# First layer's expert blocks of 128 rows instead of 256, and register reads four at a time

## The chip, the cores and the metric

The kernel runs on one core of one Trainium2 chip, in one launch. The metric is the device time of an execution in microseconds (us). The trace is that of one profiled execution.

## What is computed

The reference is a small vision tower of two layers: a patch embedding of 128 images (64 patches and a class token each, 65 x 128 = 8320 tokens of 128 numbers), then per layer an attention-like mixing and a mixture of experts of which each token uses two. The change lies in the first layer's experts, which compute:

```
xt = x.reshape(-1, d)                                   # 8320 tokens, d = 128
sel = jax.nn.sigmoid(xt @ expert_sel.T)                 # E = 32 experts
sel_val, sel_idx = jax.lax.top_k(sel, TOP_K)            # TOP_K = 2
w = jnp.zeros((T, E)).at[jnp.arange(T)[:, None], sel_idx].add(sel_val)
h = jax.nn.relu(jnp.einsum('td,edh->teh', xt, keys))    # hidden 128
out = jnp.einsum('teh,te,ehv->tv', h, w, values)
```

The second layer has 16 experts of hidden size 512 with biases and an exact gelu, again two a token.

## The kernel before, in words

The kernel runs in stages. In the first one groups of 520 tokens are embedded, mixed by attention and routed. Routing gives each of a token's two choices a row (132 numbers: the normalized token, the place where its result belongs, gate, spread and mean), and POOL scatters these rows into a list per expert in DRAM, `lists_L` (line 1551). When all are counted, DVE and PE make a table of blocks, `t_entry`, one integer a block that holds the expert and the first row. Since an expert's count is seldom a multiple of the block size, one block's worth of pad rows is written behind each expert's list: `pads`, lines 402 to 416, half of the experts by SP and half by ACT, each position read from the table `t_fr` into a register with `value_load` (line 412).

Then come the **expert blocks**. `Layer` fixes their size (256 rows for both layers) and their number: the most blocks that 16640 rows can need, rounded up to the unroll of 8, which is 96 in the first layer and 80 in the second. The number does not depend on the data; blocks beyond the last real one work on a dummy place. Eight buffers (`wblk`, `xblk`, `yblk`, index u) are used in turn. Every engine runs the same loop over blocks, 8 to a round, in program order:

- SP (`load`, lines 427 to 436) reads the block's table entry into a register (line 429), derives expert and row by register arithmetic, waits until the results that left buffer u eight blocks earlier have landed (`y_out[u]`), and issues two DMAs: the expert's weights (line 433, 128 KB in the first layer) and the block's rows (line 434, 132 KB). Both count up `blk_in[u]`.
- PE (`step`) does, for block i: transposes of block i + 2 (`t1`, line 626), which wait for `blk_in`; the first product of block i + 1 (`t2`, line 637); the second product of block i (`t3`, line 656). As PE works in order, `t3` of block i stands behind the transposes of block i + 2.
- ACT copies the transposed tile out of PSUM (line 796).
- DVE does relu of block i + 1 (line 1335), restores the rows of block i from spread and mean (line 1356, one instruction for each 128 rows) and adds the gated product (line 1375, one for each 128 rows).
- POOL (`send_results`) scatters the results into `results_L` (line 1565, one indirect DMA for each 128 rows), which counts up `y_out[u]`.

A block has Q = block / 128 such sub-tiles, 2 before. In the second layer relu is replaced by gelu and the first product is split in three passes (line 641).

After the blocks SP waits for all results (line 459) and loads them for the middle stage (line 441), which mixes, normalizes and routes for the second layer; then the second layer's pads and blocks, and the sum of each token's two results to the output.

Of the kernel before, what the change touches and what calls it, by code (L numbers as in the profile page):

```python
# [39 lines left out]
TOP = 2  # L40
# [126 lines left out]
class BlockSignals:  # L167


    def __init__(self, sem, i0, j0, y0, first=None):  # L170
        self.i0, self.j0, self.y0 = i0, j0, y0
# [12 lines left out]

def build(nc, a, out):
    ctx = ExitStack()
    with ctx:
# [156 lines left out]
        K = {"L0": BlockSignals(sem, 0, 0, 0)}  # L344
        K["L1"] = BlockSignals(sem, L0.blocks, L0.blocks // NB, 16 * L0.Q * L0.blocks // NB, K["L0"])

# [70 lines left out]
        def sp_blocks(sp, l):  # L417
# [8 lines left out]

            def load(u, j):
# [18 lines left out]
        def _(sp):  # L446
# [11 lines left out]
            for u in range(NB):  # L458
                sp.wait_ge(K["L0"].y_out[u], 16 * L0.Q * L0.blocks // L0.unroll)

# [5 lines left out]
            for u in range(NB):  # L466
                sp.wait_ge(K["L1"].y_out[u], K["L1"].y0 + 16 * L1.Q * L1.blocks // L1.unroll)

# [8 lines left out]
        def _(pe):  # L477
# [129 lines left out]
            def expert_blocks(l):  # L607
# [14 lines left out]
                def t1(u, j, n):  # L622
                    b, jj = turn(u, n, j)
                    pe.wait_ge(k.blk_in[b], 32 * (k.j0 + jj + 1))
# [38 lines left out]
                rounds = l.blocks // U  # L663
# [4 lines left out]
                def step(u, j, last):  # L668
                    if not (last and u + 2 >= U):
                        t1(u, j, 2)  # L670
                    if not (last and u + 1 >= U):
                        t2(u, j, 1)
                    t3(u, j, 0)
                for u in range(U):
                    step(u, 0, False)
                with pe.Fori(1, rounds - 1) as j:
                    for u in range(U):
                        step(u, j, False)
                for u in range(U):
                    step(u, rounds - 1, True)  # L680


# [89 lines left out]
        def _(act):  # L772
# [131 lines left out]
            def expert_blocks(l):  # L904
# [25 lines left out]
                def high(u, j, n):  # L930
                    i = U * j + u + n
                    act.wait_ge(k.blk_in[(u + n) % U], 32 * (k.j0 + j + (u + n) // U + 1))
# [9 lines left out]
                for u in range(U):  # L942
                    for f, lead in works:
                        f(u, 0, lead)
                with act.Fori(1, l.blocks // U - 1) as j:
                    for u in range(U):
                        for f, lead in works:
                            f(u, j, lead)
                for u in range(U):
                    for f, lead in works:  # L950
                        if u < U - lead:
                            f(u, l.blocks // U - 1, lead)
# [81 lines left out]
        def _(dve):  # L1034
# [290 lines left out]
            def expert_blocks(l):  # L1325
# [34 lines left out]
                def gated(u, j):  # L1360
# [4 lines left out]
                    dve.wait_ge(k.y_out[u], k.y0 + 16 * l.Q * j)  # L1365
                    y = ps[:, 6 + p2, 0:l.Q * D].rearrange("p (q d) -> p q d", q=l.Q)
                    if l.FC > 1:
                        dve.tensor_tensor(yblk[u][:, :, :], y,  # L1368
# [3 lines left out]
                        y = yblk[u][:, :, :]  # L1372
# [8 lines left out]
                def step(u, j, last):  # L1381
                    if not (last and u + lead >= U):
# [4 lines left out]
                for u in range(U):  # L1387
                    step(u, 0, False)
                with dve.Fori(1, l.blocks // U - 1) as j:
                    for u in range(U):  # L1390
                        step(u, j, False)
                for u in range(U):
                    step(u, l.blocks // U - 1, True)
# [239 lines left out]
```

## Time and profile before

| what | value |
|---|---|
| runs of the kernel | 1355.03, 1352.3, 1352.3 us; median 1352.3 |
| the profiled execution | 1354.35 us |
| its span, first to last instruction | 1352.6 us |
| mean granted TensorE clock | 0.836 |
| PE busy | 1024.7 us, 76% |
| DVE busy | 914.6 us, 68% |
| POOL busy | 700.3 us, 52% |
| ACT busy | 499.8 us, 37% |
| moved by DMA | 226.72 MB, mean 168 GB/s |

The busy shares are means over stages that differ much; what binds a stage is seen in that stage alone. The page's "idle before" gives what an engine waited for, and a name with q behind it (SPq) is an engine's own sequencer, which issues DMAs and is not counted as busy.

### The profile page before, as it was taken

What the parts mean: (1) busy time and instruction counts of PE and PEld (TensorE: products, weight loads), DVE (VectorE), ACT (ScalarE), POOL (GpSimd) and SP (SyncE); (2) the same over time, 40 slices, a digit from 0 to 9 for tenths busy, and PEclk for the clock granted to TensorE, in tenths of its full rate; (3) what the DMA queues carried; (4) which work ended last, traced back from release to release, by engine and by line L of the source; (5) the groups of instructions that cost most, each with busy time, mean ns of one, the idle gap of its engine ahead of it and who ended that gap; (6) DMA issues with size and microseconds to landing.
All of it is one profiled execution on the core that took longest, in us unless ns stands there. A gap on an engine that the chain in (4) does not pass through costs nothing.

```text
span 1352.6 us, 23759 instructions
## 1 busy us (share of the span) xinstructions
PE 1024.7 (76%) x6272; PEld 851.1 (63%) x6272; DVE 914.6 (68%) x3546; ACT 499.8 (37%) x1416; POOL 700.3 (52%) x698
## 2 busy tenths in 40 slices
PE   6999999999996326666665377777619999999920
PEld 3576666666665225555554367677618999999920
DVE  1587787787786426666665488888727888888832
ACT  1344444344353001111111255555405666656610
POOL 1033553553453517777777047777763555555520
PEclk8999999999997567888787666666658999999965
DMA  9656656566600265444442323332147777777648
GB/s 372 253 194 215 215 209 210 212 212 209 217 24 21 83 176 149 147 144 141 147 146 67 80 71 73 82 80 60 42 129 262 246 244 249 249 235 244 218 106 273
DMA packets 113697, 226.72 MB, mean 168 GB/s; under 512 B 21144, under 2 KB 87771, under 8 KB 107266
## 3 DMA queue, kind: packets, MB, share of 16 engines
q1 hardware_dynamic: 79424, 181.38, 41.5%
q0 software_dynamic: 21504, 34.73, 8.4%
q10 hardware_dynamic: 12714, 9.99, 2.5%
q8 instruction: 21, 0.34, 0.1%
q14 instruction: 34, 0.28, 0.1%
HBM read 180.32 MB, written 51.66 MB: 172 GB/s over the span
## 4 chain that ended last, share of the span: by engine, by line
PE 59%; DMA 11%; DVE 8%; issue 8%; ACT 6%; POOL 5%; SPq 2%; POOLq 0%; DVEq 0%; ACTq 0%
PE ps L656 11%; PE ps L641 9%; PE ps L493 7%; PE ps L735 5%; PE ps L490 5%; POOL results_L L1565 4%; PE ps L738 4%; DMA xin<-results_L 4%; DMA results_L<-xin 3%; DMA xin<-lists_L 3%; ACT ntok L983 2%; PE ps L554 2%; PE ps L626 2%; PE ps L511 2%; PE ps L538 2%
## 5 line engine op out<-in xcount | busy, mean ns | idle before, releaser
L1551 POOL DMA_INDIRECT lists_L<-rows,slots x270 | 302.0, 1119 | 358.5 <-issue 358.2
L1565 POOL DMA_INDIRECT results_L<-xin x352 | 343.6, 976 | 219.8 <-DVE xin L1375 142.7
L656 PEld LDWEIGHTS ps<-xin,hTb 128*128 128x128 f32 x1664 | 221.8, 201 | 9.7 <-DVE hTb L1335 0.3
L656 PE MATMUL ps<-xin,hTb 128*128 128x128 f32 x1664 | 225.7, 284 | 0.1
L493 PE MATMUL ps<-xin,w_emb 128*128 128x512 f32 x384 | 181.4, 605 | 10.3 <-DMA xin<-in_x_main 10.3
L626 PE MATMUL ps<-ident,xin 128*128 128x128 f32 x352 | 82.7, 322 | 134.8 <-DMA xin<-lists_L 134.5
L925 ACT ACTIVATE hTb<-ps,xin 128x256 f32<-128x256 f32 x320 | 125.6, 476 | 107.0 <-PE ps L641 107.0
L626 PEld LDWEIGHTS ps<-ident,xin 128*128 128x128 f32 x352 | 43.2, 156 | 155.5 <-DMA xin<-lists_L 155.2
L796 ACT ACTIVATE xTb<-ps 128x256 f32<-128x256 f32 x96 | 36.9, 384 | 238.9 <-PE ps L626 238.9
L1335 DVE TENSOR_SCALAR hTb<-ps 128x256 f32<-128x256 f32 x96 | 40.7, 424 | 109.8 <-PE ps L637 109.7
L493 PEld LDWEIGHTS ps<-xin,w_emb 128*128 128x128 f32 x384 | 68.2, 193 | 68.9 <-issue 58.6
L1356 DVE TENSOR_SCALAR xin<-xin 128x128 f32<-128x128 f32 x352 | 111.2, 366 | 0.0
L735 PE MATMUL ps<-ntok,w_emb 104*104 104x128 f32 x160 | 49.1, 431 | 67.0 <-ACT ntok L983 67.0
L641 PE MATMUL ps<-x_hi,x_lo 128*128 128x256 f32 x320 | 97.8, 306 | 0.0
L641 PE MATMUL ps<-x_lo,x_hi 128*128 128x256 f32 x320 | 91.2, 285 | 0.0
L641 PE MATMUL ps<-x_hi 128*128 128x256 f32 x320 | 90.9, 284 | 0.0
L735 PEld LDWEIGHTS ps<-ntok,w_emb 104*104 104x104 f32 x160 | 37.9, 290 | 68.8 <-ACT ntok L983 43.3
L637 PE MATMUL ps<-xTb,xin 128*128 128x256 f32 x192 | 74.4, 478 | 0.0
L1375 DVE SCALAR_TENSOR_TENSOR xin<-ps,xin 128x128 f32<-128x128 f32 x192 | 58.5, 346 | 12.5
L1368 DVE TENSOR_TENSOR xin<-ps,xin 128x256 f32<-128x256 f32 x80 | 34.0, 425 | 42.4 <-PE ps L656 42.3
L796 ACT ACTIVATE x_hi<-xin 128x512 fp32r<-128x512 f32 x80 | 51.7, 646 | 29.3 <-DMA xin<-lists_L 29.3
L641 PEld LDWEIGHTS ps<-x_lo,x_hi 128*128 128x128 f32 x320 | 62.1, 194 | 0.0
(196 smaller groups left out, 2204.7 us busy)
## 6 DMA issues: line engine op xcount, KB each, us to landing
xin<-in_x_main SPq DMA_DIRECT2D x48, 1536.0 KB, 6.9
xin<-in_w_L SPq DMA_DIRECT2D x80, 578.0 KB
xin<-lists_L SPq DMA_DIRECT2D x176, 132.0 KB
xin<-results_L SPq DMA_DIRECT2D x32, 520.0 KB
xin<-in_w_L SPq DMA_DIRECT2D x96, 128.0 KB
results_L<-xin POOLq DMA_INDIRECT x352
lists_L<-rows,slots POOLq DMA_INDIRECT x270
out<-xin ACTq DMA_DIRECT2D x16, 260.0 KB
```

Source lines behind the costliest of these rows:

```text
L490: mm = pe.matmul(psE[h], w[:, n, :], x[:, n, :], start=False, stop=False, skip_group_check=True)
L493: mm = pe.matmul(psE[h], w_emb[:, k, :], xin[h][c][:, n, :], start=(k == 0), stop=False, skip_group_check=True)
L626: mm = pe.transpose(ps[:, (u + n) % 2, q * 128:(q + 1) * 128], xblk[b][:, q, 0:D], ident[:, :])
L637: mm = pe.matmul(bank_h(p2, f), wblk[b][:, cols_f], xTb[p2][:, 0:n_tok], start=True, stop=True)
L641: mm = pe.matmul(bank_h(p2, f), w[p2][:, cols_f], x[p2], start=(n2 == 0), stop=(n2 == 2), skip_group_check=True)
L656: mm = pe.matmul(o, hTb[p2][:, f, q * 128:(q + 1) * 128], w2[:, f * D:(f + 1) * D], start=(f == 0), stop=(f == l.FC - 1))
L735: mm = pe.matmul(o, m[:, t, 0:ROWS], ntok[:, t, :], start=True, stop=(t == 0), skip_group_check=True)
L796: return act.activation(dst, src, ACT.Copy)
L925: ins = act.activation(hTb[p2][:, f, 0:l.block], ps[:, 2 + 2 * p2 + f // 2, f % 2 * l.block:(f % 2 + 1) * l.block], ACT.Gelu, bias=b1)
L1356: ins = dve.tensor_scalar(xblk[u][:, q, 0:D], xblk[u][:, q, 0:D], xblk[u][:, q, SPREAD:SPREAD + 1], xblk[u][:, q, MEAN:MEAN + 1], ALU.mult ...
L1551: pool.indirect_dma_start(out=lists[l.name], out_offset=bass.IndirectOffsetOnAxis(ap=slots_of(l, g, h)[:, t, k:k + 1], axis=0), in_=buf[:, ...
L1565: pool.indirect_dma_start(out=results[l.name], out_offset=bass.IndirectOffsetOnAxis(ap=xblk[u][:, q, PLACE:PLACE + 1].bitcast(U32), axis=0 ...
```

## The change

The first layer's blocks have 128 rows (Q = 1). Their number is no longer rounded up to a multiple of 8: it is 161 in the first layer (80 in the second, as before). The loops do a first round of 8, the inner rounds, and then the last whole round and the remaining block written out. Since 161 is no multiple of 8, the counts of the semaphores that both layers share are kept for each buffer. The block tables and the pad positions are read into registers four at a time, in both layers. In the second layer nothing else changes. A pad is now 128 rows in the first layer.

```diff
-        most = (TOKENS * TOP + experts * (block - 1)) // block
+        self.blocks = (TOKENS * TOP + experts * (block - 1)) // block
         self.unroll = unroll
-        self.blocks = -(-most // unroll) * unroll
+        self.rounds = self.blocks // unroll
+        self.turns = [len(range(u, self.blocks, unroll)) for u in range(unroll)]
...
-L0 = Layer(1, "L0", 32, 128, 256)
+L0 = Layer(1, "L0", 32, 128, 128)
...
         def rounds(eng, l, body):
 
-            for u in range(l.unroll):
-                body(u, 0)
-            with eng.Fori(1, l.blocks // l.unroll) as j:
-                for u in range(l.unroll):
+            U = l.unroll
+            for i in range(U):
+                body(i, 0)
+            with eng.Fori(1, l.rounds - 1) as j:
+                for u in range(U):
                     body(u, j)
+            for i in range(U * (l.rounds - 1), l.blocks):
+                body(i % U, i // U)
...
+        def several(engine, where, most):
+
+            return nc.values_load_multi_w_load_instructions(where, engines=[engine], min_val=0, max_val=most)[1]
...
             with eng.Fori(0, l.E // 8) as e:
-                for u in range(4):
-                    at = eng.value_load(tb.fr[0:1, bass.ds(half * (l.E // 2) + 4 * e + u, 1)], min_val=0,
-                                        max_val=l.E * l.room - l.block)
+                engine = mybir.EngineType.SP if half == 0 else mybir.EngineType.Activation
+                for at in several(engine, tb.fr[0:1, bass.ds(half * (l.E // 2) + 4 * e, 4)], l.E * l.room - l.block):
...
             def load(u, j):
                 i = l.unroll * j + u
-                entry = sp.value_load(tb.entry[0:1, bass.ds(i, 1)], min_val=0, max_val=l.E * l.step - 1)
+                if u % 4 == 0:
+                    n = min(4, l.blocks - i) if isinstance(i, int) else 4
+                    for m, value in enumerate(several(mybir.EngineType.SP, tb.entry[0:1, bass.ds(i, n)], l.E * l.step - 1)):
+                        held[m] = value
+                entry = held[u % 4]
                 e, r = entry // l.step, entry % l.step
 
-                sp.wait_ge(k.y_out[u], k.y0 + 16 * l.Q * j)
+                sp.wait_ge(k.y_out[u], k.y0[u] + 16 * l.Q * j)
```

On SP's queue, at the head of the first layer's inner loop, one block before reads (t_entry is the block table, xin_0 the weight buffer, xin_2 the row buffer, y_out the semaphore of the results that left the buffer):

```order
L429 TENSOR_LOAD t_entry
L429 ISA x2
L432 REGISTER_ALU
L433 ISA [waits y_out0]
L433 DMA xin_0<-in_w_L 128x256
L434 ISA
L434 DMA xin_2<-lists_L 128x264
L429 ISA
L429 TENSOR_LOAD t_entry
L429 ISA x2
L433 ISA [waits y_out1]
```

and now:

```order
L413 TENSOR_LOAD t_entry
L413 ISA x8
L451 REGISTER_ALU
L452 ISA [waits y_out0]
L452 DMA xin_0<-in_w_L 128x256
L453 ISA
L453 DMA xin_2<-lists_L 128x132
L452 ISA [waits y_out1]
L452 DMA xin_0<-in_w_L 128x256
L453 ISA
L453 DMA xin_2<-lists_L 128x132
```

A load with two ISA instructions (a bounds check and an assertion) stood before every block; now one load and eight of them stand before every fourth, and the row DMA has 132 instead of 264 numbers a partition.

On POOL's queue the first layer's scatters before (x16 is the first round, x2 one block of the loop, of which eight stand in a round):

```order
L1565 DMA results_L<-xin_2 16640x128 x16
L397 UNCONDITIONAL_BRANCH
L397 ISA
L1565 DMA results_L<-xin_2 16640x128 x2
L1562 REGISTER_ALU
```

and now:

```order
L1564 DMA results_L<-xin_2 16640x128 x8
L401 UNCONDITIONAL_BRANCH
L401 ISA
L1564 DMA results_L<-xin_2 16640x128
L1561 REGISTER_ALU
...
L1564 DMA results_L<-xin_2 16640x128 x9
```

One scatter a block stands where two stood, and nine blocks follow the loop.

## Rows read from the trace of the kernel before

**Rows 1.** Busy time by stage; the stages are stretches of the span in us

```profile
core 0: us, PE busy (x) PEld busy (x) DVE busy (x) ACT busy (x) POOL busy (x), PEclk, DMA share, GB/s
...
462.00:491.00 29.00, 1.29 (x8) 0.61 (x8) 2.36 (x14) 0.00 (x0) 9.94 (x10) 0.50 0.67 201
491.00:749.00 258.00, 160.26 (x768) 130.93 (x768) 151.06 (x484) 38.16 (x97) 187.28 (x192) 0.80 0.45 133
749.00:1010.00 261.00, 164.35 (x920) 158.13 (x920) 191.85 (x1142) 116.23 (x450) 160.11 (x160) 0.61 0.30 76
1010.00:1301.00 291.00, 277.72 (x2400) 277.06 (x2400) 230.64 (x640) 168.57 (x401) 156.34 (x160) 0.98 0.71 230
```

**Rows 2.** POOL's scatters: ns min/median/max, first and last start; as a group in 510:730

```profile
L1565 POOL DMA_INDIRECT results_L<-xin x192: 971/972/1300, 501.8 to 746.4; - x192
...
L1565 POOL DMA_INDIRECT results_L<-xin x173 | 168.4, 974 | 52.7 <-issue 47.3 <-DVE xin L1375 5.5
```

**Rows 3.** Waits (total, times, longest): PE in 491:749, SP in 510:730, SP in 1009:1305

```profile
PE ps L626 <- DMA xin<-lists_L: 111.0, 81, 29.5
...
SPq L433 <- DMA results_L<-xin: 58.9, 82, 2.1
...
SPq L433 <- DMA results_L<-xin: 120.6, 42, 6.8
```

**Rows 4.** Timeline of SP: start us, us, engine, line, op, out<-in

```profile
491.53 0.36 SPq L433 DMA_DIRECT2D xin<-in_w_L  x1
492.13 0.39 SPq L434 DMA_DIRECT2D xin<-lists_L  x1
493.33 0.33 SPq L433 DMA_DIRECT2D xin<-in_w_L  x1
493.88 0.33 SPq L434 DMA_DIRECT2D xin<-lists_L  x1
495.02 0.33 SPq L433 DMA_DIRECT2D xin<-in_w_L  x1
...
506.96 0.33 SPq L433 DMA_DIRECT2D xin<-in_w_L  x1
507.50 0.33 SPq L434 DMA_DIRECT2D xin<-lists_L  x1
508.75 0.33 SPq L433 DMA_DIRECT2D xin<-in_w_L  x1
...
511.20 0.33 SPq L433 DMA_DIRECT2D xin<-in_w_L  x1
```

**Rows 5.** SP's instructions by line in 515:730: duration ns min/median/max, first and last start

```profile
L429 SPq FUSED_REGOPS  x157: 52/152/158, 515.2 to 727.1; - x157
L429 SPq TENSOR_LOAD <-t_entry x84: 263/274/477, 514.8 to 726.8; - x84
L429 SPq SEQ_ASSERT  x84: 18/18/18, 515.4 to 727.3; - x84
...
L433 SPq FUSED_REGOPS  x84: 89/91/96, 516.1 to 729.4; - x84
L433 SPq DMA_DIRECT2D xin<-in_w_L x84: 331/333/342, 516.3 to 729.5; - x84
...
L434 SPq FUSED_REGOPS  x84: 73/75/83, 516.7 to 729.9; - x84
L434 SPq MOVE xin<-lists_L x83: 29/29/29, 516.8 to 726.2; - x83
L434 SPq DMA_DIRECT2D xin<-lists_L x83: 332/333/333, 516.8 to 726.3; - x83
```

**Rows 6.** DVE's groups in 510:730: count, busy us, mean ns, idle before

```profile
L1356 DVE TENSOR_SCALAR xin<-xin 128x128 f32<-128x128 f32 x172 | 53.3, 367 | 0.0
L1375 DVE SCALAR_TENSOR_TENSOR xin<-ps,xin 128x128 f32<-128x128 f32 x172 | 52.4, 346 | 11.2
...
L1335 DVE TENSOR_SCALAR hTb<-ps 128x256 f32<-128x256 f32 x86 | 36.5, 425 | 73.1 <-PE ps L637 73.0
```

**Rows 7.** Timeline of one block's way, all engines

```profile
508.27 0.97 POOL L1565 DMA_INDIRECT results_L<-xin  x1 [0.30 <-issue]
...
509.89 0.69 PE L626 MATMUL ps<-ident,xin 128*128 128x128 f32 x2 [1.50 <-DMA xin<-lists_L]
...
510.37 1.06 PE L637 MATMUL ps<-xTb,xin 128*128 128x256 f32 x2
...
511.23 1.06 PE L656 MATMUL ps<-xin,hTb 128*128 128x128 f32 x4
...
512.54 0.61 DVE L1375 SCALAR_TENSOR_TENSOR xin<-ps,xin 128x128 f32<-128x128 f32 x2
```

**Rows 8.** Timeline, end of the stage: the last scatter, the middle stage's first loads

```profile
746.37 0.97 POOL L1565 DMA_INDIRECT results_L<-xin  x1 [0.30 <-issue]
...
748.62 12.33 SPq L441 DMA_DIRECT2D xin<-results_L  x4
```

**Rows 9.** Pads: timeline, then SP's waits before the blocks of either layer

```profile
463.86 19.72 SPq L414 DMA_DIRECT2D lists_L<-padrows  x16
463.88 19.04 ACTq L414 DMA_DIRECT2D lists_L<-padrows  x16
...
SPq L424 <- DMA lists_L<-padrows: 6.4, 1, 6.4
...
SPq L424 <- DMA lists_L<-rows,slots: 6.9, 1, 6.9
```

More of the change, by code:

```diff
@@ L167, with __init__ @@
 class BlockSignals:
-    def __init__(self, sem, i0, j0, y0, first=None):
-        self.i0, self.j0, self.y0 = i0, j0, y0
+    def __init__(self, sem, before=None, first=None):
+        self.i0 = before.blocks if before else 0
+        self.j0 = before.turns if before else [0] * NB
+        self.y0 = [16 * before.Q * j0 if before else 0 for j0 in self.j0]
         if first is None:
@@ L343, in build @@
         S = {l.name: LayerSignals(sem, halves, l.name) for l in (L0, L1)}
-        K = {"L0": BlockSignals(sem, 0, 0, 0)}
-        K["L1"] = BlockSignals(sem, L0.blocks, L0.blocks // NB, 16 * L0.Q * L0.blocks // NB, K["L0"])
+        K = {"L0": BlockSignals(sem)}
+        K["L1"] = BlockSignals(sem, L0, K["L0"])
         m_in = halves("m_in")
@@ L393, in rounds, with beyond @@
         def rounds(eng, l, body):
-            for u in range(l.unroll):
-                body(u, 0)
-            with eng.Fori(1, l.blocks // l.unroll) as j:
-                for u in range(l.unroll):
-                    body(u, j)
+            U = l.unroll
[3 more added lines that the diff above has]
+                for u in range(U):
+                    body(u, j)
+            for i in range(U * (l.rounds - 1), l.blocks):
+                body(i % U, i // U)
+        def beyond(l, u, j, n):
+            return isinstance(j, int) and l.unroll * j + u + n >= l.blocks
+        def several(engine, where, most):
+            return nc.values_load_multi_w_load_instructions(where, engines=[engine], min_val=0, max_val=most)[1]
         def pads(eng, l, half):
@@ L458, in _ @@
             for u in range(NB):
-                sp.wait_ge(K["L0"].y_out[u], 16 * L0.Q * L0.blocks // L0.unroll)
+                sp.wait_ge(K["L0"].y_out[u], 16 * L0.Q * L0.turns[u])
             def load_mid(g, h, j):
@@ L466, in _ @@
             for u in range(NB):
-                sp.wait_ge(K["L1"].y_out[u], K["L1"].y0 + 16 * L1.Q * L1.blocks // L1.unroll)
+                sp.wait_ge(K["L1"].y_out[u], K["L1"].y0[u] + 16 * L1.Q * L1.turns[u])
             def load_end(g, u, j):
@@ L623, in t1 @@
                     b, jj = turn(u, n, j)
-                    pe.wait_ge(k.blk_in[b], 32 * (k.j0 + jj + 1))
+                    pe.wait_ge(k.blk_in[b], 32 * (k.j0[b] + jj + 1))
                     for q in range(l.Q):
@@ L661, in i_par @@
                     return (u + n) % 2
-                rounds = l.blocks // U
                 t1(0, 0, 0)
@@ L666, in expert_blocks, with step @@
                 t2(0, 0, 0)
-                def step(u, j, last):
-                    if not (last and u + 2 >= U):
+                def step(u, j):
+                    if not beyond(l, u, j, 2):
                         t1(u, j, 2)
-                    if not (last and u + 1 >= U):
+                    if not beyond(l, u, j, 1):
                         t2(u, j, 1)
                     t3(u, j, 0)
[L674 to L680, printed above, removed]
+                rounds(pe, l, step)
             def step(g, h, j, ahead_a, ahead_e):
@@ L931, in high @@
                     i = U * j + u + n
[L932 removed]
+                    act.wait_ge(k.blk_in[(u + n) % U], 32 * (k.j0[(u + n) % U] + j + (u + n) // U + 1))
                     if not (isinstance(i, int) and i < 2):
@@ L941, in expert_blocks, with step @@
                         f(0, 0, n)
-                for u in range(U):
+                def step(u, j):
                     for f, lead in works:
[L944 to L947, printed above, removed]
+                        if not beyond(l, u, j, lead):
                             f(u, j, lead)
[L949 to L952, printed above, removed]
+                rounds(act, l, step)
             pads(act, L0, 1)
@@ L1371, in gated @@
                         dve.wait_ge(y_biased, i + 1)
-                        y = yblk[u][:, :, :]
+                        y = yblk[u][:, 0:l.Q, :]
                     dve.wait_ge(restored, k.i0 + i + 1)
@@ L1379, in expert_blocks, with step @@
                 f, lead = (relu, 1) if l is L0 else (xT, 2)
-                def step(u, j, last):
-                    if not (last and u + lead >= U):
+                def step(u, j):
+                    if not beyond(l, u, j, lead):
                         f(u, j, lead)
@@ L1386, in expert_blocks @@
                     f(0, 0, n)
[L1387 to L1393, printed above, removed]
+                rounds(dve, l, step)
             expert_blocks(L0)
```

5 lines of the change are left out of this document (3 added, 2 removed).

## The prediction

> **What bounds the kernel now.** I first cut the span into stages [rows 1]. The change touches the expert blocks of the first layer (491 to 749 us of the span) and the stretch before them in which the pad rows are written (462 to 491); the last layer's blocks (1010 to 1301) get only the new way of reading registers. In the touched stage the stage table shows no full compute engine: PE is busy 160 of 258 us, DVE 151, ACT 38. POOL is busy 187. Its group of instructions [rows 2] says more: 192 scatters with a median of 972 ns, the first at 501.8 and the last at 746.4. (746.4 - 501.8) / 191 = 1.28 us from one to the next, so only the 0.30 us between an end and the next start separates them [rows 2], and POOL's queue is never empty for long. **The stage is 192 scatters long**: 2.56 us a block. PE waits for loads [rows 3], but these loads are late only because SP waits for a buffer until POOL's scatters out of it have landed (58.9 us of waits, each short) [rows 3]. DMA engines are 45% busy [rows 1].
>
> Behind POOL stands SP. While buffers were still free, SP issued a block's loads every 1.69 us (491.53, 493.33, 495.02) [rows 4]; inside the loop, with one more address computation, 506.96 to 508.75 is 1.79 us [rows 4]. That is well under 2.56, and far over 1.28.
>
> **Blocks.** Before, 96 blocks of 256 rows, two scatters each: 192. Now 161 blocks of 128, one scatter each: 161. At 1.28 us POOL would need 206 us instead of 246, 40 less. The question is who can feed a block every 1.28 us.
>
> **SP per block.** The medians of the loop [rows 5] put a weight DMA of 333 ns, 75 ns of register operations and 29 ns of move, and then the row DMA's 333 ns. From one start to the other is 0.55 us (506.96 to 507.50) [rows 4], so three gaps take 0.11. The way back without a table read is 0.33 + 0.09 + 0.03 + 0.11 = 0.57. Two DMAs cost 1.12 us, whatever their size, since the issue times are those of both shapes. The table read is the rest: 1.79 - 1.12 = 0.67 us, made of 52 + 274 + 152 + 18 ns [rows 5] and four gaps of 0.04 to 0.05. Of this, 0.40 (address, load) is now paid once in four blocks, but the bounds check (152 + 18 ns and two gaps of 0.05, 0.27 together) is paid for each value: the order rows show one load and eight ISA instructions behind it, where a load had two. Group: 0.40 + 4 x 0.27 = 1.48, which is 0.37 a block and **1.49 us in all**. If part of the 152 ns is the wait for the loaded register, the second to fourth checks cost about what other register operations do (73 to 91 ns) [rows 5]: group 1.2, block 1.42. The trace has no load of four values; that it costs what a load of one does is my assumption, and four loads is its other bound. The check's median is 152 and its longest 158 ns while the loads spread from 263 to 477 [rows 5], which speaks for a fixed cost. I take **1.47 us a block**, near the upper end. The range for this cost alone is 1.38 (all four checks as short as the 52 ns one) to 1.50.
>
> So SP becomes the bound in POOL's place, with 1.47 against 1.28.
>
> The Trainium skill, DMA: Bandwidth & Descriptors, section on latency and other measured facts, gives a `tensor_load` a floor of about 600 ns, to be amortized by unrolling four times. The whole read here, checks included, is 0.57 to 0.67 us; were all of it such a floor, four would share it, and the block would be 1.12 + 0.15 = 1.27. My sum stands on the rows, in which almost half of it is checks that multiply.
>
> **The others at 1.47.** DVE: 0.42 + 0.37 + 0.35 us even with the relu at its full 256 columns [rows 6], and about 0.1 of hop, is under 1.3. PE at its slower pace took 0.48 + 0.86 + 1.06 for a block (from 509.89 to 510.37, to 511.23, and the last four matmuls) [rows 7]; with half the columns about 1.2. POOL has 0.19 to spare. ACT is far from it.
>
> **The loop through eight buffers.** PE's step i first transposes block i + 2, so block i cannot finish before the load of i + 2, and load i + 8 waits for block i's scatter: the ring holds six blocks of latency. From rows: 0.55 between the two issues, 2.39 from the row DMA to the transpose (507.50 to 509.89) [rows 4, 7], 3.26 from there to the end of the gated sum (512.54 + 0.61) [rows 7], of which I estimate 1.1 goes with half the columns; 0.25 to POOL, 0.97 for one scatter, 1.96 from its end to SP's next issue (508.27 + 0.97 to 511.20) [rows 4, 7]. That is 8.3 us, or 1.38 a block. It fits under 1.47, with only 0.09 to spare; before, a second scatter and the wider tiles made it about 10.7 against 15.3, and the slack sat as a queue before POOL.
>
> **The sum**, from the first load to the first load of the middle stage, which was 491.53 to 748.62, 257.1 us [rows 4, 8]. Now: 160 x 1.47 = 235.2 for the issues, then the last block: 0.55 + 2.3 + three DVE steps of about 1.1 + 1.2 for the scatter + 1.3 until it has landed (746.37 + 0.97 to 748.62) [rows 8] = 8.8. 244.0, so **-13.1 us**.
>
> Pads: sixteen on SP and sixteen on ACT took 19.7 and 19.0 us, then SP waited 6.4 for the last to land [rows 9]. Each group of four now saves three times address and load, 3 x 0.40 = 1.2, four groups **-4.8 us**, as issue sets the pace. The wait of 6.4 I leave, since the transfer of the spans from ACT's queue moves forward along with it. Ends: 0, if transfers set the pace (DMA is 67% busy there [rows 1]), and -9, if the halved bytes also shorten the last wait. In the last layer the pads are covered: SP waited for POOL's scatters into the lists there, not for pads [rows 9]. And its blocks are PE's (277.7 of 291 us busy [rows 1]): no gain. Before the first load of each layer three more checks are paid: 2 x 0.8 = **+1.6**.
>
> Total -13.1 - 4.8 + 1.6 = -16.3. The profiled execution took 1354.35 us, 2.05 over the median 1352.3; 1354.35 - 16.3 = 1338.05, and against the median **1336**.
>
> **Rivals.** With P for the time of a block, everything is 160 x P + 8.8 - 257.1 - 3.2.
> *A, POOL stays the bound*: SP costs 1.28 or less. For it: the bare durations, 0.05 + 0.27 + 4 x 0.07 with checks of 52 + 18 ns, give 0.60 for a group, or 1.27 a block. Against it: the gaps are in every row. P = 1.28: -46.7, **1306**. 8%. It is also where the rule of the Trainium skill above would lead.
> *B, the ring binds, slower than before*: 161 blocks fetch 128 KB of weights each instead of 96, and the bytes asked for rise from 266 KB per 2.56 us to 199 KB per 1.47. In the last layer, with DMA 71% busy [rows 1], SP's waits for landed scatters reached 6.8 us, where they reached 2.1 in the first [rows 3]; so landings stretch under load. The ring decides once it is over 6 x 1.47 = 8.8 us, 0.5 more than I have; no gain is left at P = 1.57, a ring of 9.4. P = 1.60, 1.3 us of added latency, gives +4.5, **1357**. Against it: packets of 528 bytes instead of 1056 should cost less engine time, and I expect DMA at 60 to 65% only. 13%, of it 8 slower, 5 about the same.
> The same page of the Trainium skill has HBM access at 0.2 us on average and 2 us at high load, and a fixed cost of about 2 us for a DMA whatever its size, which speaks against smaller blocks. The trace agrees on the fixed cost: the 1.96 us above.
> *C, the read by fours saves nothing*: four loads' time behind one instruction. P = 1.12 + 0.67 = 1.79, no gain at the pads: about +42, **1394**. The single instruction in the order speaks against it. 3%.
>
> **Numbers.** My own case, SP at 1.38 to 1.53, has 76%. A measurement of this kernel can tell about 0.2%, 2.7 us, from no change; P = 1.57 less or more 0.02 is "same". Faster: 76 + 8 = 84%; same 5%; slower 8 + 3 = 11%. The range 1318 to 1347 is P = 1.36 to 1.54; it leaves out A, C and most of B.
>
> **What would show it.** SP's two issues per block 0.55 apart and, each four blocks, a hole of about 2.0 us, with few and short waits for landed scatters; POOL waiting for DVE before nearly every scatter, 0.2 us on average over the usual 0.3; 161 scatters from about 497 to 730; pads issued in 15 us. I am wrong if SP still waits before most blocks (then the ring or POOL binds, and POOL's gaps tell which), if the four checks take clearly other than 1.1 us, or if the DMA share passes 70%.

## The result, and the profile after

The changed kernel took 1358.29 us (median of 5 runs, 1357.1 to 1360.51), the kernel before 1352.83 beside it. The ratio is 1.0039, 95% interval 1.0025 to 1.0054: **slower by 0.4%**, where 1336 was forecast with 84% on faster. The profiled execution took 1357.1 us over a span of 1355.2, against 1354.35 and 1352.6, so the two spans may be set against each other directly: +2.6 us.

The stages of the changed kernel; 483 and 752 are where its own loads begin, the other cuts and the columns are those of [rows 1]:

```profile
462.00:483.00 21.00, 1.48 (x6) 0.50 (x6) 1.83 (x8) 0.00 (x0) 9.77 (x10) 0.50 0.68 170
483.00:752.00 269.00, 176.89 (x805) 150.30 (x805) 147.93 (x487) 45.89 (x162) 156.76 (x161) 0.65 0.54 151
752.00:1010.00 258.00, 159.25 (x920) 152.82 (x920) 191.74 (x1142) 116.05 (x450) 159.65 (x160) 0.63 0.31 77
1010.00:1301.00 291.00, 277.65 (x2400) 277.00 (x2400) 230.26 (x640) 168.34 (x401) 154.96 (x160) 0.98 0.70 230
```

POOL did give up its 31 scatters: 156.76 us busy instead of 187.28 [rows 1]. The stage became longer all the same. From first load to the middle stage's first load it took 269.1 us instead of 257.1 (**+12.0**). The pads gave **-8.2** (first load at 483.32 instead of 491.53 [rows 4]). The middle stage, the second layer's blocks and the end, cut at their first loads in the same way, gave -0.8, -0.9 and +0.5. Sum +2.6.

The pads in the timeline of SP, then the first load (start us, us, engine, line, operation):

```profile
463.30 13.96 SPq L427 DMA_DIRECT2D lists_L<-padrows  x16
483.32 0.36 SPq L452 DMA_DIRECT2D xin<-in_w_L  x1
```

The issue of sixteen took 13.96 us instead of 19.72 [rows 9]: -5.8. It began 0.56 earlier, and the stretch behind it, up to the first load, shrank from 7.95 to 6.06.

One stretch of SP's loop, from block u = 1 of a round to the head of the next; L452 is the weight DMA, L453 the row DMA:

```profile
561.73 0.33 SPq L452 DMA_DIRECT2D xin<-in_w_L  x1
...
562.85 0.33 SPq L452 DMA_DIRECT2D xin<-in_w_L  x1
563.41 0.33 SPq L453 DMA_DIRECT2D xin<-lists_L  x1
563.98 0.33 SPq L452 DMA_DIRECT2D xin<-in_w_L  x1
564.53 0.33 SPq L453 DMA_DIRECT2D xin<-lists_L  x1
566.58 0.33 SPq L452 DMA_DIRECT2D xin<-in_w_L  x1
567.14 0.33 SPq L453 DMA_DIRECT2D xin<-lists_L  x1
567.71 0.33 SPq L452 DMA_DIRECT2D xin<-in_w_L  x1
568.26 0.33 SPq L453 DMA_DIRECT2D xin<-lists_L  x1
568.95 0.33 SPq L452 DMA_DIRECT2D xin<-in_w_L  x1
...
570.71 0.33 SPq L452 DMA_DIRECT2D xin<-in_w_L  x1
571.27 0.33 SPq L453 DMA_DIRECT2D xin<-lists_L  x1
573.87 0.33 SPq L452 DMA_DIRECT2D xin<-in_w_L  x1
```

A block without a read is 1.13 us (562.85 to 563.98), the one with a group of four 2.60 (563.98 to 566.58), and the one behind the loop's end 3.16 (570.71 to 573.87): the group and 0.57 more. The steps of 1.24 and 1.76 between 567.71 and 570.71, into blocks u = 6 and u = 7, hold waits. In the whole stage 21 of SP's 22 waits for a buffer stand before one of these two blocks. The weight loads start at 483.32 (first) and 741.58 (last), so P, the time of a block, was 258.26 / 160 = **1.614 us**; the forecast was 1.47.

The parts of a read, from the view of line 413 in 510:700 (duration ns min/median/max), and the loop's end, line 401:

```profile
L413 SPq FUSED_REGOPS  x131: 52/147/161, 513.5 to 696.9; - x131
L413 SPq SEQ_ASSERT  x116: 18/18/18, 514.1 to 697.1; - x116
L413 SPq TENSOR_LOAD <-t_entry x29: 295/300/458, 513.5 to 695.8; - x29
```
```profile
L401 SPq ALU_OP  x14: 37/37/37, 519.9 to 689.2; - x14
L401 SPq COMPARE_BRANCH  x14: 45/45/45, 520.0 to 689.3; - x14
L401 SPq FUSED_REGOPS  x14: 59/59/59, 520.2 to 689.6; - x14
```

The waits of the stage: SP's in 500:730, then PE's and POOL's in 480:760 (total, times, longest), and POOL's group in 500:730:

```profile
SPq L452 <- DMA results_L<-xin: 8.7, 22, 1.1
```
```profile
PE ps L645 <- DMA xin<-lists_L: 105.8, 80, 21.9
POOL results_L L1564 <- DVE xin L1380: 86.0, 59, 16.4
POOL results_L L1564 <- issue: 34.0, 102, 0.7
```
```profile
L1564 POOL DMA_INDIRECT results_L<-xin x142 | 137.9, 971 | 93.8 <-DVE xin L1380 63.9 <-issue 29.9
```

SP's waits for landed scatters fell from 58.9 us in 82 [rows 3] to 8.7 in 22. POOL's gaps grew: 93.8 / 142 = 0.66 us, where they were 0.30 [rows 2]. PE waits for loads, and now it is not for want of a buffer but of SP. **The bound moved from POOL to SP**, as forecast, but SP needs 1.61 us for each of 161 blocks; before, 96 blocks at POOL's 2.56 held 246 us.

### The profile page after: what moved, and what is told of

Its sections match the earlier page's. It is cut to its first block, busy times and chain, and to the rows that moved or that the text cites. A ratio compares the mean times of both kernels' runs of the same rounds, so it can differ in the third digit from the quotient of the medians.

```text
span 1355.2 us, 24802 instructions
## 1 busy us (share of the span) xinstructions
PE 1034.9 (76%) x6309; PEld 864.2 (64%) x6309; DVE 911.0 (67%) x3549; ACT 507.1 (37%) x1481; POOL 668.5 (49%) x667
## 4 chain that ended last, share of the span: by engine, by line
PE 57%; DMA 12%; DVE 9%; issue 7%; SPq 7%; ACT 6%; POOL 2%; POOLq 0%; DVEq 0%; ACTq 0%
PE ps L675 11%; PE ps L660 9%; PE ps L512 7%; PE ps L509 5%; PE ps L745 5%; DMA results_L<-xin 4%; DMA xin<-results_L 4%; PE ps L748 3%; DMA xin<-lists_L 3%; PE ps L573 2%; ACT ntok L988 2%; SPq L452 2%; PE ps L530 2%; PE ps L557 2%; SPq L413 2%
## 5 line engine op out<-in xcount | busy, mean ns | idle before, releaser
L1564 POOL DMA_INDIRECT results_L<-xin x321 | 312.7, 974 | 256.3 <-DVE xin L1380 196.6
L675 PE MATMUL ps<-xin,hTb 128*128 128x128 f32 x1602 | 246.9, 296 | 0.0
L675 PEld LDWEIGHTS ps<-xin,hTb 128*128 128x128 f32 x1602 | 227.1, 213 | 0.5 <-DVE hTb L1340 0.3
L645 PE MATMUL ps<-ident,xin 128*128 128x128 f32 x321 | 100.0, 353 | 130.1 <-DMA xin<-lists_L 129.5
L645 PEld LDWEIGHTS ps<-ident,xin 128*128 128x128 f32 x321 | 49.3, 162 | 157.4 <-DMA xin<-lists_L 155.7
L806 ACT ACTIVATE xTb<-ps 128x128 f32<-128x128 f32 x161 | 44.6, 277 | 244.2 <-PE ps L645 244.2
L1340 DVE TENSOR_SCALAR hTb<-ps 128x128 f32<-128x128 f32 x161 | 46.8, 291 | 114.8 <-PE ps L656 108.7
L656 PE MATMUL ps<-xTb,xin 128*128 128x128 f32 x322 | 92.8, 387 | 0.0
L656 PEld LDWEIGHTS ps<-xTb,xin 128*128 128x128 f32 x322 | 77.9, 297 | 0.0
```

The source lines that it names most:

```text
L645: mm = pe.transpose(ps[:, (u + n) % 2, q * 128:(q + 1) * 128], xblk[b][:, q, 0:D], ident[:, :])
L656: mm = pe.matmul(bank_h(p2, f), wblk[b][:, cols_f], xTb[p2][:, 0:n_tok], start=True, stop=True)
L675: mm = pe.matmul(o, hTb[p2][:, f, q * 128:(q + 1) * 128], w2[:, f * D:(f + 1) * D], start=(f == 0), stop=(f == l.FC - 1))
L806: return act.activation(dst, src, ACT.Copy)
L1564: pool.indirect_dma_start(out=results[l.name], out_offset=bass.IndirectOffsetOnAxis(ap=xblk[u][:, q, PLACE:PLACE + 1].bitcast(U32), axis=0 ...
```

## The experiments

Two theories, and a third that mixes them. **S**: SP's own instructions set P and nothing else does. **R**: the ring of eight buffers sets it. **M**, the mixed cycle: buffer u comes back one ring latency after its load, over six blocks of SP's way; SP's way over six blocks that hold only one group of reads is short of that latency, so SP waits there, and in the other blocks it is SP's instructions that count. By M, P is neither of the two but a little over the greater.

The runs were made in groups, each with the kernel before in it. In some groups the kernel before takes 1352 us, in others 1493 to 1516; so every ratio is to the kernel before of the same group. The record gives a group of either kind the same chip number (again and again3, chip 2), so it isn't shown that the chip makes the difference. What was measured in the second kind of group was repeated in the first where it carries the argument.

### Groups in which the kernel before took 1352 us

**again3**, the changed kernel itself, no edit.

> The changed kernel itself, beside the two below. If the kernel before takes about 1352 us here, 1.004 of it; if about 1500, 0.991, with waits for landed scatters of about 1.9 us a round behind the table reads.

1357.95 us, ratio 1.0033 [1.0022, 1.0045]. First and last load at 482.5 and 742.1 us: P = 1.623. The loss is stable.

**single2**, one read a block. **twos**, the same with `per = 2`.

```diff
+            per = 1
             def load(u, j):
...
-                if u % 4 == 0:
-                    n = min(4, l.blocks - i) if isinstance(i, int) else 4
+                if u % per == 0:
+                    n = min(per, l.blocks - i) if isinstance(i, int) else per
...
-                entry = held[u % 4]
+                entry = held[u % per]
```

> Each entry read by itself. Where the kernel before takes about 1500 us: M says that the ring of buffers, which there takes over 10 us, gives back what the fours save, so this is within 12 us of the changed kernel, at P about 1.9, with waits of under 0.7 us a round. Where it takes 1352: P = 1.86, SP's own 14.9 us a round, no waits, 1.033 of the kernel before. S says +40 us over the changed kernel on either.

> Entries read two at a time in both layers: a round has four groups of 0.40 + 0.54 = 0.94 us and costs SP 8 x 1.12 + 4 x 0.94 + 0.57 = 13.3 us, 0.8 more than by fours and 1.6 less than singly, but its holes are 0.94 instead of 1.48 us. S: halfway, +16 us over the changed kernel. M, where the kernel before takes about 1500 us: six blocks in a row always hold three groups, 9.6 us of SP, under the ring of over 10: waits at most 1 us a round, and the time is within 10 us of the changed kernel, on either side. Where it takes 1352: P = 1.66, +8 us.

single2: 1397.62 us, 1.0315 [1.0296, 1.0335], 39.7 us over again3; loads from 481.9 to 781.3, P = 1.871. The view of SP's waits in 500:700 is empty. Here SP's instructions alone are the bound, and the 1.033 of theory S (and M, which gives the same where the ring has slack) lies within the interval. **Reading by fours is worth 0.25 us a block, 40 us.** Without it the blocks of 128 would lose 3%.

twos: 1378.87 us, 1.0194 [1.0173, 1.0215], P = 1.765 (480.2 to 762.5); SP waits for nothing here either. Both forecasts missed: +21 us over again3, where S had +16 and M +8 with P = 1.66. The miss is in the load itself. TENSOR_LOAD in 510:700 of single2, then of twos:

```profile
L413 SPq TENSOR_LOAD <-t_entry x101: 269/276/472, 510.7 to 699.2; - x101
```
```profile
L413 SPq TENSOR_LOAD <-t_entry x54: 470/475/562, 512.0 to 699.1; - x54
```

One value 276 ns, two 475, four 300. Two values cost more than four; I had assumed one price. Four groups that cost some 0.2 us more than the 0.94 I had are most of the miss of 8 x 0.10 us a round.

**nocheck4**, the changed kernel without the bounds check and assertion behind each value read, at the pads and in both layers.

```diff
-            return nc.values_load_multi_w_load_instructions(where, engines=[engine], min_val=0, max_val=most)[1]
+            return nc.values_load_multi_w_load_instructions(
+                where, engines=[engine], min_val=0, max_val=most,
+                skip_runtime_bounds_check_because="the table is clamped where it is made")[1]
```

> The changed kernel without the bounds checks and assertions. Where the kernel before takes 1352 us: SP's own round is 12.5 - 8 x 0.27 = 10.3 us, 1.29 a block. M: the ring of 8.6 us over six blocks then binds, P = 1.43 to 1.50, the kernel at 1328 to 1340, 0.982 to 0.991 of the kernel before, SP waiting for landed scatters before most blocks, over 1 us a round. S: P = 1.29, 1306. If PE at its lower clock level binds as in the kernel with both edits (P = 1.60): 1355. Where the kernel before takes about 1500: 0.967 to 0.973 again.

1331.87 us, ratio **0.9849 [0.982, 0.9878]**: it beats both kernels. Loads from 483.6 to 717.0: P = 1.459. Its stage in 500:700, and SP's waits there:

```profile
500.00:700.00 200.00, 138.04 (x684) 115.25 (x683) 125.38 (x410) 37.68 (x136) 132.60 (x137) 0.73 0.62 175
```
```profile
SPq L454 <- DMA results_L<-xin: 23.0, 55, 2.0
```

S said 1.29 and 1306, R nothing (the ring holds no check), M 1.43 to 1.50 and 1328 to 1340. M holds. 200 / (8 x 1.459) is 17 rounds, so SP waits 1.35 us a round and works 10.3 of 11.7, as computed; the waits stand before 55 of some 137 blocks, not before most. The ring can be measured at them. From the weight DMA of block i to that of block i + 6, where the latter waited, it took **8.5 us** (median of 53, worked out from the starts in the trace), or 1.42 a block, and in the changed kernel 8.6 (median of 19). P = 1.459 is a little over the greater of 1.42 and SP's 1.29, as M has it. The checks cost SP 0.27 us a block, but only 0.155 of it comes back.

The place of the waits bears M out too. In the changed kernel they stand before u = 6 and u = 7, where the last six blocks on SP hold one group and no loop end (8.25 us, under 8.6). In twos and single2 any six blocks take SP over 9.4 us, and there are no waits.

**order2**, PE's order in the first layer: t3 of block i first, then t2 of i + 1, then t1 of i + 2, so that a result no longer stands behind the transposes of the second block after it.

```diff
-                    if not beyond(l, u, j, 2):
+                    if l is L0:
+                        t3(u, j, 0)
+                    elif not beyond(l, u, j, 2):
                         t1(u, j, 2)
                     if not beyond(l, u, j, 1):
                         t2(u, j, 1)
-                    t3(u, j, 0)
+                    if l is L1:
+                        t3(u, j, 0)
+                    elif not beyond(l, u, j, 2):
+                        t1(u, j, 2)
```

> The changed kernel with PE's order changed alone: the second product of block i ahead of the transposes of block i + 2. Where the kernel before takes 1352 us: M says that the ring's waits (0.4 us a round) go and SP's own 12.5 us a round are left, P = 1.56 to 1.57, 8 us less than the changed kernel, but PE's chain at its lower clock level, 1.60 in the kernel with both edits, puts a floor under it: 1.60, 3 us less. S: no change. Where the kernel before takes about 1500: 0.971 again.

**both4**, both edits together.

> No checks, and PE's order changed. 0.960 to 0.964 of the kernel before where that takes about 1500 us, as in three runs; where it takes 1352, P = 1.30 to 1.45, 0.965 to 0.984, or if PE binds at its lower clock level as in those runs, 1.00.

order2: 1359.47 us, 1.0052 [1.0035, 1.0069]; P = 1.613 (481.4 to 739.4). both4: 1355.41, 1.0029 [1.0011, 1.0047]; P = 1.603 (482.5 to 739.0). So the two edits together lose what the first alone gains. 500:700 of order2, then of both4, and behind it four blocks of both4's timeline:

```profile
500.00:700.00 200.00, 177.51 (x615) 127.73 (x615) 110.24 (x369) 34.18 (x123) 119.22 (x124) 0.50 0.55 158
```
```profile
500.00:700.00 200.00, 177.58 (x620) 128.01 (x620) 111.26 (x372) 34.35 (x124) 120.01 (x124) 0.50 0.56 159
```
```profile
599.77 0.63 PE L658 MATMUL ps<-xTb,xin 128*128 128x128 f32 x2
...
600.20 0.42 PE L647 MATMUL ps<-ident,xin 128*128 128x128 f32 x1
...
600.79 0.80 PE L677 MATMUL ps<-xin,hTb 128*128 128x128 f32 x2 [0.17 <-DVE hTb L1347]
...
601.12 0.35 DVE L1387 SCALAR_TENSOR_TENSOR xin<-ps,xin 128x128 f32<-128x128 f32 x1
601.38 0.63 PE L658 MATMUL ps<-xTb,xin 128*128 128x128 f32 x2
...
602.29 0.97 POOL L1571 DMA_INDIRECT results_L<-xin  x1 [0.64 <-issue]
...
602.99 0.64 PE L658 MATMUL ps<-xTb,xin 128*128 128x128 f32 x2
...
604.66 0.64 PE L658 MATMUL ps<-xTb,xin 128*128 128x128 f32 x2
```

In both4 PE repeats every 1.61 to 1.67 us (599.77, 601.38, 602.99, 604.66), busy 177.6 of 200 us, at a granted clock of 0.50 (1.2 GHz) throughout. It no longer stops for loads, only 0.17 us a block for the relu. SP has time to spare there: it waits for landed scatters 85 times in the same window, 42.8 us in all. So **a PE chain of 1.60 us at 1.2 GHz sets the pace**. In order2 PE waits for a load only twice in the 200 us, so that the same chain sets the pace, at 1.61 a little over SP's own 1.56. But SP's waits in 500:700 of order2 are not gone, as M would have it:

```profile
SPq L452 <- DMA results_L<-xin: 6.9, 12, 1.6
```

The changed kernel has 7.2 us in 20 waits in the same stretch. The ring of order2 spans seven blocks, but at its waits it takes 9.9 us (median of 13), since PE's slower chain lies in it: from a transpose to the end of the gated sum behind it are now 2.9 us, where they were 2.0. So order2 is no test of M; what is shown is that making the ring longer this way trades it for PE.

Why PE works at the lower level there is open. In nocheck4 the mean clock was 0.73, between the two levels. That the missing stops for loads lower it doesn't follow: single2 has the old order, 59.7 us of waits for loads on PE in the same window, and 0.50 as well:

```profile
500.00:700.00 200.00, 139.98 (x531) 109.76 (x530) 98.38 (x317) 29.47 (x106) 102.93 (x107) 0.50 0.48 137
```

### Groups in which it took 1493 to 1516 us

Run earlier, in three groups. **nocheck, order, both, q256** side by side; q256 is the change without its small blocks:

```diff
-L0 = Layer(1, "L0", 32, 128, 128)
+L0 = Layer(1, "L0", 32, 128, 256)
```

> The changed kernel without the bounds check and the assertion behind each value read into a register (eight instructions fewer a group of four, 1.06 us by the changed kernel's trace). Theory M, SP's queue and the ring of buffers together: a round of eight blocks is 12.9 us now, 12.5 of SP's own issues and 0.4 of waits where the ring (8.6 us for six blocks) is longer than SP's way through six blocks. Without the checks SP's round is 10.4, the ring's six blocks stay 8.6, and the longest mixed path is the ring once and SP twice, one of them with a read: 11.8 a round, 1.48 a block. Blocks -21 us, pads and first reads about -5: near 1333. Theory S, SP alone: 1.30 a block, near 1303. Theory R, the ring alone: the blocks stay at 1.61, only the pads gain, near 1353.

> The changed kernel with PE's step in the first layer turned round: second product of block i, first product of i + 1, then the transposes of i + 2, so that block i stands behind the load of i + 1 and no longer of i + 2 and the ring holds seven blocks. Theory M: only the waits go, 0.05 us a block, SP's own 1.56 stays: -8 us, near 1350. Theory S: nothing moves, 1358. Theory R: the blocks fall to POOL's 1.28, -50 us, near 1308.

> Both edits: no checks on SP, and PE's order turned round. Theory M: SP's 1.30 a block is left and the ring of seven is shorter than SP's way through seven blocks: -50 us for the blocks and -5 before them, near 1303. Theory S: as without the checks alone. Theory R: as with PE's order alone.

> The changed kernel with blocks of 256 rows in the first layer, 96 of them: the register reads four at a time remain of the change. POOL's 192 scatters bind as before, 1.28 us each. If the pads gain by SP's issue time alone (14 us instead of 19.7, less 0.8 for the first group), the blocks start 4 to 5 us earlier and the kernel takes 1348 to 1349. If the 8.2 us by which the blocks start earlier in the changed kernel come from the reads alone, 1345. If halved pads were all of it, 1353.

Ratios 0.9671 [0.9627, 0.9714], 0.9708 [0.9646, 0.977], 0.961 [0.9566, 0.9653] and 0.9921 [0.989, 0.995]. For q256 1345 to 1353 of 1352.8 was forecast, 0.995 to 1.000; it came out a little lower. It wasn't repeated in a group of the first kind, so what the reads by four alone do for blocks of 256 rows is not measured there. Then **again, nocheck2, both2** (repeats) and **eight**, the first layer's entries read eight at a time (`per = 8 if l is L0 else 4` in the edit of single2):

> The changed kernel itself, to stand beside the experiments on the same chip, since the four runs before fell on a chip on which the kernel before takes 1493 us. Every theory expects 1.004 of the kernel before where that takes 1353 us. The profile shows whether SP's issues are again evenly 0.55 us apart.

> The changed kernel without bounds checks once more, with the changed kernel beside it. Theory M (SP and ring together): 0.98 of the changed kernel, about -25 us, 1.48 us a block. Theory S (SP alone): -55 us, 1.30 a block. Theory R (ring alone): -5 us, 1.61 a block.

> No checks, and PE's order turned round, with the changed kernel beside it. On the other chip the profile showed that the transposes came 4.5 us after the row DMA's issue instead of 2.0 and that the granted clock stayed at the lower level through the stage. Theory M: 1.30 us a block, -55 us against the changed kernel. Theory P, PE becomes the bound: with the order turned, relu stands between first and second product in each step, and at the lower clock a block takes PE over 1.5 us; then the time is near that without the checks alone.

> The changed kernel with the first layer's table entries read eight at a time, with all their checks: one address and load fewer a round on SP (0.4 us of 12.5), but all checks in one place. Theory M: SP's way through six blocks without a read is 6.7 us, so the ring's 8.6 us is bound at once, and then SP's read with 2.9 us and the loop's end come on top: 8.6 + 2.2 + 2.9 = 13.7 to 13.9 us a round, 1.73 a block, +18 us against the changed kernel though SP does less. Theory S: 12.1 us a round, -8 us. Theory R: no change.

again: 0.9907 [0.988, 0.9933], so the same two programs stand the other way round there. nocheck2 0.9661 [0.9622, 0.9701], both2 0.9592 [0.9556, 0.9629], eight 1.0046 [1.0027, 1.0065]. Last **single, nocheck3, both3, both8** (both and eight together):

> The changed kernel, but each table entry is read by itself again, in both layers; blocks stay 128 rows. It says what the reading by fours is worth. If SP's own instructions set the pace (theory S), a round of eight is 8 x (1.12 + 0.67) + 0.57 for the loop end = 14.9 us against 13.0, P = 1.86, no waits for landed scatters left: 160 x 0.25 = 40 us slower than the changed kernel, about 1.033 of the kernel before where the changed one is 1.004, and about 1.02 where it is 0.991. The mixed cycle (theory M) gives nearly the same, since six blocks with singles take SP 11 us, over the ring's 8.6. If the ring of buffers alone set the pace (theory R), 0 to +10 us, since it has no table read in it.

> The changed kernel without the bounds checks and assertions on the values read, a repeat to see whether its gain over the changed kernel (0.991 to 0.967 of the kernel before, where both were run together) stands at other times or places too. Where SP's instructions start as promptly as in the changed kernel's first trace: SP's own round is 12.5 - 8 x 0.27 = 10.3 us, 1.29 a block, under the ring's 8.6 / 6 = 1.43, so M gives P = 1.43, -29 us, 0.983 of the kernel before; S gives 1.29, -52 us, 0.965; if checks cost nothing, 1.004.

> No checks, and PE does the transposes of block i + 2 behind the second product of block i + 1 and of block i ahead of them. With prompt instructions: the ring no longer holds back (the result of block i does not stand behind the transposes of block i + 2), POOL could do 1.28 and SP 1.29; PE at its lower clock level needs about 1.2 plus its waits. M: P = 1.30 to 1.45, 0.965 to 0.984 of the kernel before, 3 to 20 us under the kernel without checks alone. If it is PE that binds as in the earlier run (1.63 a block, granted clock 0.50 through the whole stage), 0.96 where the changed kernel is 0.991, and about 1.00 where that is 1.004.

> As the last, and the first layer's entries read eight at a time. A group of eight saves one address and load in eight blocks, 0.40 us, 0.05 a block. With checks in, eight at a time cost 20 us, since the group is a hole that the ring can't bridge. M: without checks the group is 0.40 + 8 x 0 and the order of PE has slackened the ring, so nothing is lost: -8 to 0 us against the kernel with reads by fours. S: -8. If reading by eights is bad by itself, however short the group: +10 or more.

0.9977 [0.9957, 0.9998], 0.9734 [0.9708, 0.976], 0.9641 [0.9614, 0.9668], 0.9665 [0.9627, 0.9704]. single was to be 1.02 and was not.

What differs there is seen in again's timeline of SP. SP waits for no landing in this stretch:

```profile
600.30 0.01 SPq L452 DMA_DIRECT2D xin<-in_w_L  x1
601.75 0.70 SPq L453 DMA_DIRECT2D xin<-lists_L  x1
602.50 0.32 SPq L452 DMA_DIRECT2D xin<-in_w_L  x1
603.04 0.33 SPq L453 DMA_DIRECT2D xin<-lists_L  x1
```

Row and weight DMA stand 1.45 us apart instead of 0.55, and an issue lasts 0.70 instead of 0.33, while the view of waits in 500:700 gives SP one wait of 0.6 us. PE has gaps in again that the view puts down to nothing it waits for, 7.8 us in 8, the longest 2.5; the changed kernel's first trace (1357.1 us) has none in this window:

```profile
PE ps L645 <- issue: 7.8, 8, 2.5
```

POOL's gaps in q256 are 70.5 / 119 = 0.59 us in 515:700, behind its first scatters, for the 0.30 of [rows 2], at the same 974 ns a scatter; 34.1 of the 70.5 are waits for DVE, so its blocks come late.

So in these groups instructions of SP and PE begin late at times. Why they do, and why the changed kernel gains by it against the kernel before, no run tests. What these runs tell of the change's own mechanism is little: eight's loss of 20 us against again agrees with M's +18, but its trace has such late starts in the same places, so it proves nothing; and the four kernels with the new order of PE (order, both, both2, both3) take 6 to 28 us less than the same without it, where order2 gains none and both4 loses 24. Why is open.

A larger ring, the direct remedy, wasn't tried.

## Why the prediction was wrong

The forecast of the mechanism, POOL to SP, was right. **The step that failed is the time of a block, "1.47"**, which was 1.614: 160 x 0.144 = 23.0 of the 25.1 us by which the stage missed.

- *SP per block, reads.* The text worked out 1.49 (1.12 + 0.37) and then took 1.47. The group measured 2.60 - 1.13 = 1.47 us and two DMAs 1.13: 1.125 + 0.365 = 1.49. The sum was right and the discount was not: all four checks cost 147 to 161 ns, so next to nothing of the 152 was a wait for the load. About +0.02. (The 1.69 us that I gave for free buffers is one of two intervals; the other, 491.53 to 493.33, is 1.80. Nothing rests on it.)
- *The loop's end, left out.* A round of eight ends in an ALU operation, a compare-and-branch and a register operation (37 + 45 + 59 ns), which with the gaps around them made the block behind it 0.57 us longer on SP. It was in the trace before as well, but my interval of 1.79 (506.96 to 508.75) lay within a round, as did all the medians. 0.57 / 8 = **+0.07**. While POOL was the bound it cost nothing; now each one counts.
- *The ring.* I had 8.3 us and held it harmless under 6 x 1.47. Measured at the changed kernel's waits it was 8.6 (median of 19). The term too small is "0.25 to POOL", which was 0.85 at these waits; shorter ways from the row DMA to the transpose (2.1 for 2.39) and on to the gated sum (2.0 for 2.2) gave most of it back, and from the scatter's end to SP's next issue it was 2.1 for 1.96. In all traces of the first kind of group a scatter starts 0.30 us after the end of the one before it or 0.81 after the gated sum's end, whichever is later (within 0.1 us in 157 of the changed kernel's 160; in both4: 601.12 + 0.35 to 602.29). In the trace before the first decided in all 191, so the second could not be seen; in the changed kernel the second decides in 66 of 160. The ring is under SP's mean (8.6 / 6 = 1.43 against 1.56) and doesn't bind as a whole. But the six steps up to u = 6, or to u = 7, hold one group and no loop end, 5 x 1.13 + 2.60 = 8.25, and SP waits for what is missing (570.71 - 561.73 = 8.98 in the stretch above): 8.7 us in the 17.8 rounds of 230 us, 0.5 a round, **+0.06** a block. That averages hide this was not thought of: a block's mean against the ring's mean can have slack while a part of the round has none.
- Together: 1.49 + 0.07 + 0.06 = 1.62, measured 1.614. What failed is thus two terms put at nothing, the loop's end and the ring's wait, and a discount of 0.02.
- *Tail.* 8.8 was forecast (its terms as written add up to 8.65), 752.45 - 741.58 = 10.9 came. The gated sums of the last blocks come faster than POOL scatters, so the last stands in a queue. From the timeline of the stage's end, the last row DMA, the last transpose, DVE's last gated sum and POOL's last scatters:

```profile
742.13 0.33 SPq L453 DMA_DIRECT2D xin<-lists_L  x1
...
744.52 0.42 PE L645 MATMUL ps<-ident,xin 128*128 128x128 f32 x1
...
746.18 0.97 POOL L1564 DMA_INDIRECT results_L<-xin  x1 [0.80 <-DVE xin L1380]
747.45 1.01 POOL L1564 DMA_INDIRECT results_L<-xin  x1 [0.30 <-DVE xin L1380]
...
747.76 0.35 DVE L1380 SCALAR_TENSOR_TENSOR xin<-ps,xin 128x128 f32<-128x128 f32 x1
...
748.77 1.25 POOL L1564 DMA_INDIRECT results_L<-xin  x1 [0.30 <-issue]
750.32 0.97 POOL L1564 DMA_INDIRECT results_L<-xin  x1 [0.30 <-issue]
```

  The last gated sum ended at 747.76 + 0.35 = 748.11, and its scatter began 2.2 us later. I had let it start at once.
- *Pads.* -4.8 and +0.8 were forecast for the first load, -8.2 came: the issue -5.8, and the end of -9 ("if the halved bytes also shorten the last wait") is where it went, since SP's wait for the last pad fell from 6.4 [rows 9] to 3.7 us:

```profile
SPq L437 <- DMA lists_L<-padrows: 3.7, 1, 3.7
```

- *Other stretches.* +0.8 was forecast for the second layer's reads; its blocks came 0.9 shorter, the middle stage 0.8 shorter. PE binds the one, the other is untouched.
- Sum: +25.1 (stage), -4.2 (pads), -1.7 (last layer), -0.8 and +0.5 make the 18.9 us between -16.3 and +2.6.

**The rivals.** A, POOL stays the bound, is out: its gaps doubled. The rule of the Trainium skill (DMA: Bandwidth & Descriptors, latency and other measured facts) that went with it, a `tensor_load` of about 600 ns to be amortized by four, is not what these rows show: a load of one or four values takes 276 or 300 ns (of two 475), and the checks behind each value, 147 + 18 ns and gaps, are not shared. The checks are what stands between 1.61 and 1.46. C is out by single2. B had the right size (P = 1.60, 1357) by luck, for another cause: it took longer landings under more DMA load and a ring of 9.4 us or more, but the load was 54%, not much over 45 [rows 1] and below my 60 to 65, the row DMA's way to the transpose was no longer than the 2.39 I used (742.13 to 744.52 for the last), and the ring was 8.6. The waits of 6.8 us in the last layer, which I took for stretched landings, need none: PE is busy 277.7 of 291 us there [rows 1] and gives the buffers back at its own pace. C's price was a little high by its own formula (+40, not +42), which changes nothing. The range fell short since its upper end, 1.54, was built from the spread of the read alone, and no cost outside the quoted interval was let in; P = 1.57, "no gain left", was 0.08 from the sum.

Of what was to show it, these came: the issues 0.55 apart, a hole of 2.0 us every four blocks, few and short waits for landed scatters, pads in under 15 us. Otherwise than expected were a hole of 2.6 at the loop's end, POOL's gaps of 0.66 instead of 0.50, its waits for DVE before 59 of 161 scatters and not before nearly all, and scatters up to 750 instead of 730.

## What to carry to other kernels

When a change makes a sequencer the bound, cost a whole round of its loop, with its end, its checks and every instruction between two DMAs: an interval within the round leaves out what the old bound had hidden. Smaller tiles pay once a tile what larger ones pay half as often; here SP's 1.12 us of DMA issues, 0.37 of table read and 0.07 of loop end took more than POOL's 31 scatters gave, and taking out the checks on values that are already clamped turned 1.004 of the kernel before into 0.985. And weigh a ring of buffers against the shortest run of blocks that it spans, with the start-up of engines that will now stand idle (here 0.81 us between a sum's end and its scatter, hidden as long as POOL was behind), not against the mean.

## What the runs showed of the hardware that I had not expected

- A TENSOR_LOAD of one value took 276 ns, of two 475, of four 300 (medians of 101, 54 and 29).
- POOL began a scatter 0.30 us after the end of the one before it or 0.81 after the gated sum's end, whichever was later: 157 of 160 in the changed kernel, as many in single2, twos, nocheck4 and both4. The other three of each were late by 0.1 to 2.6 us.
- PE's busy share did not tell its clock. In 500:700 the granted clock was 0.50 at 177.5 us busy (both4, order2), 0.50 at 140 (single2) and 0.73 at 138 (nocheck4); the changed kernel had 0.65 at 133.
- The same two programs stand at 1.003 in one group of runs and at 0.991 in another, under the same chip number; in the second SP's instructions begin up to 0.7 us late with nothing waited for.
